# The product of the Mamba scan's second half with C, moved from DVE to Pool in all 16 states, with C's row copied to SBUF by ACT

## What is computed

```python
def step(h, inp):
    d, b, c, ut = inp
    dA = jnp.exp(d[:, :, None] * A)
    h = dA * h + (d * ut)[:, :, None] * b[:, None, :]
    y = jnp.einsum('bdn,bn->bd', h, c)
    return (h, y)
...
_, ys = lax.scan(step, h0, xs)
return ys.transpose(1, 0, 2) + u * D
```

## Time and profile before

| | |
|---|---|
| median of 3 runs | 4877.81 us (4872.91 to 4878.98) |
| the profiled execution's own time | 4866.22 us |
| its span in the trace | 4864.2 us |
| busy share PE / DVE / ACT / Pool | 73% / 62% / 42% / 26% |
| granted TensorE clock, mean | 0.833 |
| DVE, the scan L2097 | 512 instructions, 1.21 us each |
| DVE, the product with C, L2102 | 512 instructions, 0.69 us each |
| Pool, the inputs L1980 and additions L1993 | 512 and 256 instructions, 1.3 us each |

### The profile page before, as it was taken

The page is one execution under the profiler, slowest core; times in us unless marked ns, Lnnn a source line. Parts: engine busy times, 40 slices in busy tenths (PEclk is TensorE's granted clock), DMA queues, the critical chain, the costliest instruction groups (busy, mean ns, idle before and its releaser), DMA issues. The chain is left out here.

```text
span 4864.2 us, 69143 instructions
## 1 busy us (share of the span) xinstructions
PE 3539.3 (73%) x25546; PEld 2352.9 (48%) x25546; DVE 2997.2 (62%) x7047; ACT 2028.7 (42%) x3183; POOL 1241.7 (26%) x1568
## 2 busy tenths in 40 slices
PE   6768868566977787764886887866588788686655
PEld 4645545334665454432574554533366455453333
DVE  4535873885553785577555488377655558737834
ACT  2324445343343444444343354544433354453422
POOL 0001450550000333254000044145200014505500
PEclk7979989768988898877997998977799899887666
DMA  6020021313211012222212002122312100213121
GB/s 222 7 92 20 27 76 40 128 38 104 85 58 61 31 45 83 70 81 78 98 45 102 12 27 79 44 89 74 106 55 80 66 18 28 85 36 120 40 100 46
DMA packets 174903, 327.99 MB, mean 67 GB/s; under 512 B 13260, under 2 KB 114988, under 8 KB 173740
## 3 DMA queue, kind: packets, MB, share of 16 engines
q1 hardware_dynamic: 174572, 323.59, 19.5%
HBM read 231.87 MB, written 91.67 MB: 67 GB/s over the span
## 5 line engine op out<-in xcount | busy, mean ns | idle before, releaser
L1980 POOL TENSOR_TENSOR sb_big<-sb_big 128x512 f32<-128x512 f32 x384 | 497.7, 1310 | 275.7 <-DVE sb_big L2080 275.6
L1417 POOL TENSOR_TENSOR sb_rs<-sb_ve,sb_weights_const 128x4 f32<-128x4 f32 x112 | 113.7, 1015 | 1635.7 <-DVE sb_ve L1403 1635.7
L1864 PE MATMUL bank<-sb_big,sb_weights_const 128*128 128x512 f32 x512 | 373.4, 819 | 202.0 <-DVE sb_big L2102 201.4
L1941 ACT ACTIVATE bank<-sb_big,sb_Aneg 128x512 f32<-128x512 f32 x512 | 350.5, 687 | 391.9 <-DVE sb_big L2097 272.3
L2097 DVE TENSOR_TENSOR_SCAN sb_big<-bank,sb_big 128x512 f32<-128x512 f32 x384 | 465.2, 1212 | 4.7 <-POOL sb_big L1980 4.7
L1235 DVE TENSOR_REDUCE sb_small<-bank 128x4 f32<-128x308 f32 (+1 forms) x512 | 265.1, 524 | 318.0 <-PE bank L950 311.7
L971 PE MATMUL bank<-sb_big 128*77 128x128 bf16 (+1 forms) x2560 | 359.3, 232 | 124.7 <-issue 85.5
L971 PEld LDWEIGHTS bank<-sb_big 128*77 128x77 bf16 (+1 forms) x2560 | 272.7, 116 | 213.3 <-issue 148.3
L1120 ACT ACTIVATE sb_big<-bank 77x512 f32<-77x512 f32 (+1 forms) x352 | 208.3, 593 | 263.3 <-PE bank L992 173.8
L974 PE MATMUL bank<-sb_topT,sb_pick 128*77 128x128 bf16 (+1 forms) x2048 | 301.7, 228 | 0.0
L950 PE MATMUL bank<-sb_big 128*128 128x77 bf16 (+1 forms) x2048 | 186.3, 226 | 155.6 <-DMA sb_big<-query_parts 98.8
(11 more groups left out here) (339 smaller groups left out, 8174.2 us busy)
## 6 DMA issues: line engine op xcount, KB each, us to landing
sb_big<-query_parts SPq DMA_DIRECT2D x160, 512.0 KB, 6.6
sb_big<-state_rows SPq DMA_DIRECT2D x128, 512.0 KB, 3.8
query_parts<-sb_big SPq DMA_DIRECT2D x120, 384.0 KB, 3.3
sb_big<-key_parts SPq DMA_DIRECT2D x64, 512.0 KB, 9.0
sb_big<-context_key_parts SPq DMA_DIRECT2D x64, 308.0 KB, 3.8
key_parts<-sb_big SPq DMA_DIRECT2D x48, 384.0 KB, 4.4
context_key_parts<-sb_big SPq DMA_DIRECT2D x48, 231.0 KB, 4.1
sb_big<-masked_key_parts SPq DMA_DIRECT2D x32, 308.0 KB, 3.5
```

The source lines that it names most:

```text
L1864: pe.matmul(m.bank[s][2][:, :], m.const["ident"], M.h(s, 2 * (n % 2)), start=n == 0, stop=n == NS - 1)\
L1941: act.activation(M.dA(s, half), M.dl(s, half), ACT.Exp, scale=m.Aneg[:, NS * half + n:NS * half + n + 1])\
L1980: pool.tensor_tensor(M.h(s, 2 * (n % 2) + half), M.b_rows(s, n // 2)[:, n % 2, :], M.du(s, half), ALU.mult)\
```

## The change

Half 1's product with C goes from DVE to Pool, in every state (`on_pool` is true for all n). Pool's product reads C from SBUF: ACT copies the row from bank 1 to a new SBUF tile `c_row` (one tile per stream, 512 elements wide, at offset 5936). In detail:

- ACT gets one copy per state (128x512, PSUM to SBUF), due after both decays of the state. It waits for the row in bank 1 and, since there is one `c_row`, for Pool's product of the state before.
- DVE loses product 1. Its product 0 still reads bank 1, but now waits for ACT's copy (`sc_c`) in place of PE's matmul (`sc_bc`).
- Pool's `mamba_sum` first multiplies h by `c_row` (waits: the copy, the scan of half 1), then waits for that itself, then adds.
- PE may refill bank 1 once product 0 is done (before: product 1); product 0 itself waits for the copy.
- The signals of the quantised network are merged into those of the other feed-forward networks; they wait for the same things as before under other names.

```diff
@@ SIGNALS @@
-    ff_pe="PE: hidden tile", ff_a="ACT: hidden tile", ff_d="DVE: hidden tile", dn_pe="PE: expert's output",
+    ff_pe="PE: hidden tile or its parts", ff_a="ACT: hidden tile or its parts",
+    ff_d="DVE: hidden tile or its parts", dn_pe="PE: expert's output",
-    sc_in="Pool: a state's input", sc_y1="Pool: state added to the second half's y",
-    qf_pe="PE: quantised network", qf_a="ACT: quantised network", qf_d="DVE: quantised network",
-    qf_p="Pool: quantised network",
+    sc_in="Pool: a state's input", sc_c="ACT: a row of C is in SBUF", sc_out="Pool: state times C",
+    sc_y1="Pool: state added to the second half's y",
...
@@ class Mamba @@
+    def c_row(self, s):
+        return cut(self.m.big[s], 5936, N)
+
+    def on_pool(self, n):
+        return True
...
@@ mamba_pe, spread(n) @@
             pe.matmul(m.bank[s][1][:, :], m.sel3[0:96, row:row + 1].to_broadcast([96, 128]), M.parts(s),
                       start=True, stop=True).then_inc(*g.one("sc_bc", (way, n)))
-            free[s, 1] = ("sc_d", (way, n, "out", 1))
+            free[s, 1] = ("sc_d", (way, n, "out", 0 if M.on_pool(n) else 1))
...
@@ mamba_act @@
                 act.activation(M.dA(s, half), M.dl(s, half), ACT.Exp,
                                scale=m.Aneg[:, NS * half + n:NS * half + n + 1])\
                    .then_inc(*g.one("sc_da", (way, n, half)))
+            if M.on_pool(n):
+                yield M.at(way, 0.135) if n == 0 else M.scan_at(way, n - 1, 1.15)
+                act.wait_ge(*g.at("sc_bc", (way, n)))
+                last = [k for k in range(n) if M.on_pool(k)][-1:]
+                if last:
+                    act.wait_ge(*g.at("sc_out", (way, last[0])))
+                act.activation(M.c_row(s), m.bank[s][1][:, :], ACT.Copy).then_inc(*g.one("sc_c", (way, n)))
...
@@ mamba_sum @@
 def mamba_sum(pool, g, M, way, n):
     s = g.s
-    pool.wait_ge(*g.at("sc_d", (way, n, "out", 1)))
+    h = M.h(s, 2 * (n % 2) + 1)
+    if M.on_pool(n):
+        pool.wait_ge(*g.at("sc_c", (way, n)))
+        pool.wait_ge(*g.at("sc_d", (way, n, "scan", 1)))
+        pool.tensor_tensor(h, M.c_row(s), h, ALU.mult).then_inc(*g.one("sc_out", (way, n)))
+        pool.wait_ge(*g.at("sc_out", (way, n)))
+    else:
+        pool.wait_ge(*g.at("sc_d", (way, n, "out", 1)))
     pool.wait_ge(*g.at("mb_d", ("clear", way)) if n == 0 else g.at("sc_y1", (way, n - 1)))
-    pool.tensor_tensor(M.y1(s), M.y1(s), M.h(s, 2 * (n % 2) + 1), ALU.add).then_inc(*g.one("sc_y1", (way, n)))
+    pool.tensor_tensor(M.y1(s), M.y1(s), h, ALU.add).then_inc(*g.one("sc_y1", (way, n)))
 
 
...
@@ mamba_dve @@
                 h = M.h(s, 2 * (n % 2) + half)
                 dve.tensor_tensor_scan(h, M.dA(s, half), h, 0.0, ALU.mult, ALU.add)\
                    .then_inc(*g.one("sc_d", (way, n, "scan", half)))
+                if half == 1 and M.on_pool(n):
+                    continue
                 yield M.scan_at(way, n, 0.35 + 0.5 * half)
-                dve.wait_ge(*g.at("sc_bc", (way, n)))
+                dve.wait_ge(*(g.at("sc_c", (way, n)) if M.on_pool(n) else g.at("sc_bc", (way, n))))
                 dve.wait_ge(*g.at("sc_d", (way, n, "scan", half)))
                 dve.tensor_tensor(h, m.bank[s][1][:, :], h, ALU.mult)\
                    .then_inc(*g.one("sc_d", (way, n, "out", half)))
...
@@ quantised_pool @@
-    last.then_inc(*g.one("qf_p", "pad"))
+    last.then_inc(*g.one("proj_p", ("L3f", "pad")))
```

More of the change, by code:

```diff
@@ L1425, in turn_pe @@
     if key == "L3f":
-        pe.wait_ge(*g.at("qf_d", "r3"))
+        pe.wait_ge(*g.at("ff_d", "r3"))
     else:
@@ L2222, in quantised_pe @@
         pe.matmul(m.bank[s][k][:, :], Q.w("w1", 128 * j, 128 * j + 128), m.xT[s][:, :], start=True, stop=True)\
-          .then_inc(*g.one("qf_pe", ("h", j)))
-        free[s, k] = ("qf_a", ("h", j))
+          .then_inc(*g.one("ff_pe", ("h", j)))
+        free[s, k] = ("ff_a", ("h", j))
     for b in range(NB + 1):
@@ L2228, in quantised_pe @@
             if b == 0:
-                pe.wait_ge(*g.at("qf_a", ("hs", 3)))
+                pe.wait_ge(*g.at("ff_a", ("hs", 3)))
             if b >= 2:
@@ L2234, in quantised_pe @@
                                     m.const["ident"])
-            last.then_inc(*g.one("qf_pe", ("tok", b)))
-            free[s, b % 2] = ("qf_d", ("q1", b))
+            last.then_inc(*g.one("ff_pe", ("tok", b)))
+            free[s, b % 2] = ("ff_d", ("q1", b))
         if b >= 1:
             yield Q.time(b - 1, 0.8)
-            pe.wait_ge(*g.at("qf_d", ("q3", b - 1)))
+            pe.wait_ge(*g.at("ff_d", ("q3", b - 1)))
             g.wait_free(pe, free, s, 2)
@@ L2243, in quantised_pe @@
                                     Q.qb(s, b - 1)[:, 128 * j:128 * j + 128], m.identb[:, :])
-            last.then_inc(*g.one("qf_pe", ("back", b - 1)))
-            free[s, 2] = ("qf_a", ("qT", b - 1))
+            last.then_inc(*g.one("ff_pe", ("back", b - 1)))
+            free[s, 2] = ("ff_a", ("qT", b - 1))
     yield 0.98
     g.wait_free(pe, free, s, 3)
-    pe.wait_ge(*g.at("qf_a", ("qT", NB - 1)))
+    pe.wait_ge(*g.at("ff_a", ("qT", NB - 1)))
     for b in range(NB):
@@ L2252, in quantised_pe @@
                              m.w2t[:, 128 * j:128 * j + 128], start=j == 0, stop=j == 3)
-    last.then_inc(*g.one("qf_pe", "out"))
+    last.then_inc(*g.one("ff_pe", "out"))
     free[s, 3] = ("x_upd", "L3f")
@@ L2290, in step @@
     def step(name, last):
-        last.then_inc(*g.one("qf_d", name))
+        last.then_inc(*g.one("ff_d", name))
     def after(name):
-        dve.wait_ge(*g.at("qf_d", name))
+        dve.wait_ge(*g.at("ff_d", name))
     yield 0.02
@@ L2336, in quantised_dve @@
             if tap == 0:
-                dve.wait_ge(*g.at("qf_a", ("h", j)))
-                dve.wait_ge(*g.at("qf_p", "pad"))
+                dve.wait_ge(*g.at("ff_a", ("h", j)))
+                dve.wait_ge(*g.at("proj_p", ("L3f", "pad")))
                 ins = dve.tensor_scalar(Q.hs(s, j), src, w, None, ALU.mult)
             else:
-                dve.wait_ge(*g.at("qf_d", ("conv", j, tap - 1)))
+                dve.wait_ge(*g.at("ff_d", ("conv", j, tap - 1)))
                 ins = dve.scalar_tensor_tensor(out=Q.hs(s, j), in0=src, scalar=w, in1=Q.hs(s, j),
                                                op0=ALU.mult, op1=ALU.add)
-            ins.then_inc(*g.one("qf_d", ("conv", j, tap)))
+            ins.then_inc(*g.one("ff_d", ("conv", j, tap)))
     for b in range(NB):
         def step(name, last):
-            last.then_inc(*g.one("qf_d", (name, b)))
+            last.then_inc(*g.one("ff_d", (name, b)))
         def after(name):
-            dve.wait_ge(*g.at("qf_d", (name, b)))
+            dve.wait_ge(*g.at("ff_d", (name, b)))
         yield Q.time(b, 0.0)
-        dve.wait_ge(*g.at("qf_pe", ("tok", b)))
+        dve.wait_ge(*g.at("ff_pe", ("tok", b)))
         step("mx", dve.tensor_reduce(Q.sm(s, 4, b), m.bank[s][b % 2][:, :], AX.X, ALU.max))
@@ L2378, in quantised_dve @@
         if b >= 2:
-            dve.wait_ge(*g.at("qf_pe", ("back", b - 2)))
+            dve.wait_ge(*g.at("ff_pe", ("back", b - 2)))
         step("q3", dve.tensor_scalar(Q.qb(s, b), Q.qa(s, b), ROUND, None, ALU.subtract))
     yield 0.96
-    dve.reciprocal(Q.sm(s, 8), Q.sm(s, 7)).then_inc(*g.one("qf_d", "inv2"))
-    dve.wait_ge(*g.at("qf_d", "inv2"))
-    dve.tensor_scalar(Q.sm(s, 8), Q.sm(s, 8), m.wsc[:, 3:4], None, ALU.mult).then_inc(*g.one("qf_d", "f"))
+    dve.reciprocal(Q.sm(s, 8), Q.sm(s, 7)).then_inc(*g.one("ff_d", "inv2"))
+    dve.wait_ge(*g.at("ff_d", "inv2"))
+    dve.tensor_scalar(Q.sm(s, 8), Q.sm(s, 8), m.wsc[:, 3:4], None, ALU.mult).then_inc(*g.one("ff_d", "f"))
     yield 0.99
-    dve.wait_ge(*g.at("qf_d", "f"))
-    dve.wait_ge(*g.at("qf_pe", "out"))
+    dve.wait_ge(*g.at("ff_d", "f"))
+    dve.wait_ge(*g.at("ff_pe", "out"))
     for b in range(NB):
```

12 lines of the change are left out of this document (6 added, 6 removed).

## The result

The changed kernel takes **4948.32 us** (median; 4941.67 to 4953.65), the kernel before on the same chip 4875.36 (medians of 4 runs each). The ratio is 1.0150, 95% interval 1.0132 to 1.0168: 73 us slower (64 to 82), against a forecast of 16. The direction was right; the time lies 3 us above the range.

A forecast was written before the change was run, and what follows sets the result against it. DVE was taken to set the pace in the Mamba stretches, Pool second. Terms: 5 + 27 - 10 - 10 - 24 - 4 = 16 us lost, on 4877.8: 4894 us, range 4838 to 4945 (the forecast's own 4868 to 4925).

The forecast's parts named there:

- The bound: In the Mamba stretches DVE mostly sets the pace, Pool second; a removed DVE product counts 0.60 us.
- Rival 4: Pool doesn't lead in the stretches, its steps hide: 124 us gained, 4754; chance 0.03.
- A step of Pool: Pool's list per state after the change, two inputs, product and addition, by spacing of starts: 5.06 us.
- Term 1: Steps between additions: 126 of 240 become Pool-led, 63 us longer; 114 lose 0.60 each, 68 us; net 5 us gained.
- Term 2: Slack between steps: DVE, ready early in Pool-led steps, helps a following DVE-led one; 27 us gained, bounds 0 to 54.
- Terms 3 and 4: DVE's last lines wait for Pool's later last addition, 10 us lost; beside the expert network DVE waits for ACT, 10 lost.
- Term 5: Work queued behind the new waits, ACT's exponentials and the attention's chain, comes later: 24 us lost, bounds 0 and 125.
- Rival 2: Lock-step with the attention: the delayed copy holds up exponential, sums, L1256 and scan; 58 lost for 24, 4928; chance 0.15.
- Term 6: DVE instructions with two SBUF inputs (L2342) and Pool's meet more often side by side: 4 us lost, bounds 0 and 40.
- Rivals 2 and 3: Attention lock-step, 4928, chance 0.15; and the port, Pool products holding up two-SBUF-input DVE instructions, 38 for 4, 4928, chance 0.05.
- The signs: In stretches: DVE busy 11 us less, Pool 20 more, over 85% in middle two; steps never under 5.0; first kind 3 to 6 shorter.

The follow-up runs named there:

- e16: The change, but Pool multiplies only the last 256 columns and DVE the first 256, copy ahead of product 0, Pool not held: 4881.83 us, ratio 1.0018.
- e9: e7 without Pool's product: copies stay, Pool adds the state without C, so y lacks that product: 4799.38 us, ratio 0.9856.
- e7: e5 with Pool held after its reciprocal deviation until DVE has written the layer norm's normalised tile: 4882.25 us, ratio 1.0017.
- e6: The change with Pool held after its reciprocal deviation until DVE has written the layer norm's normalised tile: 4929.79 us, ratio 1.0117.
- e5: The change with a second tile for C's row in odd states and the copy put behind product 0: 4892.93 us, ratio 1.0039.
- e2: The change with product 0 waiting for PE's row alone and ACT's copy behind product 0, still one row tile: 4896.36 us, ratio 1.0055.
- e12: Kernel before, both products on DVE, no copy, plus an unused Pool product of two tiles per state that nobody awaits: 4942.04 us, ratio 1.0140.
- e14: e12 with Pool held behind the layer norm while DVE normalises: 4919.89 us, ratio 1.0100.
- e13: The change with Pool multiplying only the last 256 columns, DVE the first 256, half-row copy behind product 0, Pool held: 4853.35 us, ratio 0.9962.
- e4: Kernel before, both products on DVE, no copy, plus an unused Pool product of one tile by itself per state: 4879.28 us, ratio 1.0016.
- e15: e4 with a second small Pool operation of 48 columns, one tile read twice, behind the first: 4929.07 us, ratio 1.0122.

## Why the prediction was right and wrong

The runs make a budget of the 73 us, each line the difference of two timed kernels (each difference uncertain by 10 to 13 us). They add up to 73 by their making; taken in another order they would come out otherwise, as e16 shows:

| step | us | from |
|---|---|---|
| 256 products off DVE | -70 | e9 |
| Pool's product, copy behind product 0, two rows, Pool held | +78 | e7 - e9 |
| the waits: copy ahead of product 0, one row | +49 | e6 - e7 |
| the blocking of L1408 | +16 | change - e6 |

- **The bound.** DVE "mostly sets the pace" was half right. Each product taken off it is worth 0.27 us, not 0.60, even where Pool does not take it over (e9). Rival 4 priced that case at 124 gained; it is 70.
- **A step of Pool** at 5.06 us: right to the hundredth, and so was the choice of spacing over durations.
- **Term 1** (5 gained). For the kernel that it describes, without coupling, it was near, within the 15 us to which a trace's split is good: by its counts the kinds of stretch should change by about -27, +14, +10 and -2 us; e5 shows -20, +18, +4, +9, e7 -22, +8, -2, +5. That short steps become 5.06 and eat the relief is what the steps of e9 and e7 show.
- **Term 2** (27 gained). No run shows a gain that could be it. Terms 1 to 4 together forecast 12 gained, e7 has 8 lost. The loop itself was read well: in the changed kernel's eight last steps, where Pool has no inputs to make, it takes 3.95 us for the 3.8 of the sum. That the queues of ACT and DVE use up the slack elsewhere, since the sum counted both as free the moment they were wanted, is my reading and wasn't tested.
- **Terms 3 and 4** (10 each) weren't tried alone; e7 contains them.
- **Term 5, the step that failed most:** 24 forecast, 46 to 49 measured (change against e2; e6 against e7), each uncertain by some 10. The mechanism was there, my place for it was not. I charged ACT's exponentials and L1256, one case in five; DVE's wait before L1256 went only from 173.2 to 183.6 us. What waits is product 0 itself, 120.6 us, with DVE's list, y's matmul and the transposes behind it on PE. The 146.6 us of refills that I put on the other side went as told (PE's row L1859 waits 1.1 us for DVE in the changed kernel), but no gain from it can be seen, and it wasn't tried alone. Rival 2 read the rows wrongly too: the maxima's steps stand in 40 of the 240 steps, not in 96.
- **Term 6, mis-sized:** 4 forecast, 11 to 16 measured for L1408 alone (19 between e12 and e14). The prediction looked only at instructions with two SBUF inputs. Those of the earlier trace rows did become 10.5 us longer in all (862 to 1025 ns each), at a price that no run separates. The ones that are hit hardest have one: the layer norm's L1408, 4 x 0.34 us, 5.21 us beside a full Pool. It would follow from a rule I had cited only in part: the Trainium skill (SBUF — State Buffer, Who interferes with whom) counts VectorE's fast two-port modes as well as two SBUF inputs. The trace shows the blocking, 1.12 to 5.21 us; that L1408 runs in such a mode, no run here shows.
- **The sum.** Against the budget terms 1 to 4 miss 20 us, term 5 misses 25 and term 6 12: together the 57 between 16 and 73. The direction was forecast, but it hung on small terms: without the waits and L1408's blocking the change is hardly slower than before (e7).
- **The range.** Rivals 2 and 3 were priced each alone at 4928, both together would have given 4962; Pool's list, the waits and the port come together, since each grows with Pool's list (e16 against e13: 27 us, where the whole product has 65). The upper end of 4945 added no two of them. And terms 2 and 5 moved by half, 13.5 and 12 us, span 4868 to 4920, not to 4925.
- **The signs.** Pool at 20 us more per stretch, the floor of 5.0 (but for eight last steps) and the chain L2124, L1956, L2008 came as told. Pool over 85% came in the third stretch (86%), not in the second (78%), and DVE's 11 us less in none. The first kind of stretch shorter by 3 to 6 us did not come (0.5 a pass): it is 5 a pass in e2, so the waits took it.

**Open.** Why Pool's list costs 8 us up to 4.7 us a state and 60 more for the next 0.22 (e4, e12), and not more for another 0.23 (e15). Between e4 and e12 it is 0.23 us of time a state, just the added occupancy, as if nothing carried any of it; which work sets the edge I didn't find. The mean granted clock of the timed executions differs as well, 0.834 in e4 and 0.823 in e12 (0.832 before), and how much of the 60 us goes with it is open. So is how e16's 27 us divide between waits and port.

## What to carry to other kernels

An engine that looks half idle may have all of its slack inside the loop of one step. Look at the single steps and count those that its new list would be longer than, not at the mean: before the change 41 of 240 steps were shorter than the 4.56 us of the half product (e13), 62 shorter than the 5.06 of the whole one. Here half of the product was a gain and the whole a loss, and the half gained only with the copy behind product 0 and Pool held. When work moves to an engine, order the new copy behind what already uses its source, so that the old chain doesn't hang on the new one. When several hazards grow with the same cause, here Pool's list, price them together.
